# Constants at the ends of stages, half the batches normalised in the adding stage, and changed orders in five stages

## The chip, the cores and the metric

The kernel runs on one core of a Trainium2 chip. The metric is the device time of one execution in microseconds (us). The core's engines are PE (TensorE, matrix products), DVE (VectorE), ACT (ScalarE), POOL (GpSimd) and SP (SyncE, which issues most transfers). Each runs its own list and waits on semaphores. A difference of about 0.5% can be told from none.

## The reference

Twelve sublayers act on x of 8 batches × 128 tokens × 256 channels, float32, with a layer norm without weights ahead of each:

```
for layer in 0..3:
    x = x + attn(layernorm(x))
    x = x + cross_attn(layernorm(x), ctx)
    x = x + ffn(layernorm(x))
```

The sublayers differ. What the change touches of them:

```
# L0 ffn
x_dq = clip(round(x * scale_x), -128, 127) / scale_x         # per token
w_dq = clip(round(w / gamma_w), -1, 1) * gamma_w
bit_linear = x_dq @ w_dq.T + b
out = bit_linear(silu(bit_linear(x, gate)) * bit_linear(x, val), out)
# L2 cross attention: per head of 16 channels
q = ln(x @ Wq + bq); k = ln(ctx @ Wk + bk); softmax(q k / 4) v
# L3 attn: a state space layer with 64 heads, chunks of 128
L = exp(where(i >= j, cs_i - cs_j, -inf)); Y = sum_j (C_i . B_j) L_ij dt_j x_j ; (Y + D x) * silu(z) -> rms norm -> W_out
# L3 ffn: 8 experts of 1,2,3,4,1,2,3,4 chunks of 128 hidden units, and a shared one
h = x @ down; every expert on every token, masked h for experts not chosen
out = sum_e gate_e * (gelu(gelu(h_e) @ w1_e + b1_e) @ w2_e + b2_e) + 0.1 * shared; out @ up + gelu(x) @ core
```

## The kernel before

All of x lies in SBUF for the whole run. Each sublayer is a stage (L0a, L0x, L0f, L1a … L3f: attention, cross attention, feed forward), a block of its own in which every engine has a list written by hand; at the end of a stage all engines meet at a barrier, and semaphores are cleared. The order of work on each engine is that in which the code is written.

A stage begins with `Norm` (line 120). DVE aggregates the statistics of 8 batches (L152), ACT takes the root (L203), DVE the reciprocal and the negative mean (L187, L189), and then ACT scales batches 0, 1, 2, 6 (L212) and DVE 3, 4, 5, 7 (L147). PE turns each batch with two 128x128 transposes (L240), and ACT and DVE copy them out (L219, L181). While PE waits, it multiplies a constant by the identity into an unused bank (`idle`, L225): two products 512 columns wide at the start and narrower ones between the first batches. Where the stage before adds its result to x on DVE in four parts of two batches, `measure` (line 260) puts the statistics of the two batches behind each add (L264). `Norm.tensor` and these adds stand around every stage boundary.

In L0f (line 1113) the weights are ternary and x is rounded to integers. Eight batches run through a loop: PE makes gate and value (L1195), DVE scales them and adds the biases (L1312, L1322), ACT applies silu (L1246), DVE multiplies (L1343), takes the absolute maximum (L1345) and the scales, ACT rounds (L1268, L1272), PE turns and multiplies by the output weights.

In L2x (line 2220) queries and keys of eight batches are centred (L2370), squared, summed (L2349), given a reciprocal root (L2301 on ACT) for batches 0 to 3 and 4 to 7, normalised (L2358) and turned on PE (L2266) in two halves. ACT copies the keys (L2326) and DVE the queries (L2365).

In L3a (line 2498) a loop runs over 32 pairs of heads. Per pair PE adds a causal mask to four banks (`differences`, L2671: the identity times a 128x512 mask, and L2675: products of 32 rows that add the differences of cumulated steps), ACT takes their exponential (L2813), DVE multiplies (L2930), and PE forms the projections of a later pair as three products of rounded halves (L2728), the outputs y (L2690), transposes (L2740) and the sum over pairs in banks 0 to 3 (L2701), which stands half before and half behind the differences.

In L3f (line 3273) a hidden unit is one product of a 128x128 block of w1 with 512 tokens (L3362, plain float32), n counts units, and unit n uses bank n%4 of four. ACT applies gelu from the bank (L3451), PE multiplies by w2 (L3400) and DVE weighs by the gates and sums (L3502). Before unit 4 PE forms what experts give for a masked h (L3372), turns the idle weights (L3379) and multiplies them (L3385), and DVE starts the sum with that (L3491).

## Time and profile before

| | us |
|---|---|
| median of 3 runs | 1903.01 (1902.84 to 1909.08) |
| the profiled execution | 1902.77, its span 1901.0 |
| mean granted TensorE clock in the span | 0.952 |
| PE / DVE / ACT / POOL busy | 1667.9 / 1177.0 / 921.2 / 449.8 |
| the L3a loop | about 445 of the span (1110 to 1555) |
| L0x, L0f and L3f begin at | 111.8, 247.8 and 1780.1 |

Busy shares are means over twelve stages with different limits, so each place is read by its timeline. A granted clock of 0.50 means 1.2 GHz, 1.00 means 2.4 GHz. A matmul record's end is modelled; the distance between starts tells what a product costs. A plain float32 product 512 columns wide stands as two records.

### The profile page before, as it was taken

Reading aid. Unit: us, or ns where it says so; the run is one execution under the profiler, and the core shown is the slowest. Engines: PE = TensorE matmul, PEld = TensorE weight load, DVE = VectorE, ACT = ScalarE, POOL = GpSimd, SP = SyncE. Lnnn points to the kernel's source line nnn. Section 1 sums busy time; section 2 is a strip of 40 time slices with the busy share of each in tenths; the row PEclk is TensorE's granted clock in tenths of the full one; section 3 lists DMA queues with packets and bytes.
Section 4 is the critical chain, followed back from the end, with each engine's and each line's share of the span. In section 5 each row is a group of like instructions: output and inputs, shape, how many; then the busy total and the mean of one; then the engine's idle time right before and its main releaser. Section 6 shows DMA issues by size and latency. Waiting matters only on the chain. (4 is left out here: it accounts for less than half of the span.)

```text
span 1901.0 us, 37141 instructions
## 1 busy us (share of the span) xinstructions
PE 1667.9 (88%) x13775; PEld 1293.5 (68%) x13778; DVE 1177.0 (62%) x2317; ACT 921.2 (48%) x1953; POOL 449.8 (24%) x501
## 2 busy tenths in 40 slices
PE   7978855789999799976878879999999988999898
PEld 4766733558888646643667647777777766888676
DVE  3676688656666612226545678888888865666622
ACT  2445576246666411111344456767676644555432
POOL 1020011023333032221300224545445530000200
PEclk9999977899999999998989989999999989999899
DMA  2020000300010172221000000101010112110000
GB/s 101 3 92 3 4 30 27 118 18 26 25 33 25 68 317 44 46 50 38 15 2 28 18 17 26 33 25 33 25 33 25 28 39 100 34 33 25 1 1 22
DMA packets 27679, 77.58 MB, mean 41 GB/s; under 512 B 2992, under 2 KB 14896, under 8 KB 25392
## 3 DMA queue, kind: packets, MB, share of 16 engines
q1 hardware_dynamic: 23488, 70.91, 10.9%
q0 software_dynamic: 4080, 5.13, 1.7%
q8 instruction: 77, 1.26, 0.3%
q14 instruction: 34, 0.28, 0.0%
HBM read 62.75 MB, written 13.28 MB: 40 GB/s over the span
## 5 line engine op out<-in xcount | busy, mean ns | idle before, releaser
L2575 DVE SCALAR_TENSOR_TENSOR arena<-bank,arena 128x508 f32<-128x508 f32 (+2 forms) x204 | 151.5, 743 | 27.9 <-ACT arena L2571 15.6
L2701 PE MATMUL bank<-L3a_wo,L3a_y_gated 128*128 128x256 f32 x512 | 124.0, 386 | 0.0
L2930 DVE TENSOR_TENSOR L3a_decays<-L3a_decays,L3a_cb_masked 128x512 f32<-128x512 f32 x128 | 94.7, 802 | 43.4 <-ACT L3a_decays L2813 43.4
L225 PE MATMUL bank<-const 128*128 128x512 f32 (+1 forms) x156 | 79.6, 644 | 42.5 <-PEq L65 42.5
L2813 ACT ACTIVATE L3a_decays<-bank 128x512 f32<-128x512 f32 x128 | 66.1, 602 | 97.0 <-PE bank L2675 97.0
L2728 PE MATMUL bank<-L3a_xnT_high,L3a_w_high 128*128 128x512 f32 x256 | 105.8, 413 | 1.5 <-ACT L3a_decays L2813 1.5
L2701 PEld LDWEIGHTS bank<-L3a_wo,L3a_y_gated 128*128 128x128 f32 x512 | 92.4, 190 | 17.6 <-issue 7.3
L2728 PE MATMUL bank<-L3a_xnT_high,L3a_w_low 128*128 128x512 f32 x256 | 99.8, 390 | 0.0
L2728 PE MATMUL bank<-L3a_xnT_low,L3a_w_high 128*128 128x512 f32 x256 | 99.7, 389 | 0.0
L1932 PE MATMUL bank<-L1f_experts,xnT 128*128 x184 | 84.6, 604 | 0.9 <-DVE xnT L2035 0.7
L3027 POOL TENSOR_TENSOR arena<-arena 128x1024 f32<-128x1024 f32 x32 | 81.3, 2541 | 14.7 <-ACT arena L2820 14.7
L1983 ACT ACTIVATE arena<-bank 128x512 f32<-128x512 f32 x23 | 13.8, 598 | 141.2 <-PE bank L1932 141.2
L225 PEld LDWEIGHTS bank<-const 128*128 128x128 f32 x156 | 32.4, 230 | 69.7 <-issue 69.7
L787 ACT ACTIVATE L1x_p<-bank,L1x_minus_max,L1x_q_scale 128x128 f32<-128x128 f32 x128 | 56.7, 453 | 31.9 <-DVE L1x_minus_max L1780 31.9
L2690 PE MATMUL bank<-L3a_decays,L3a_dtx 128*64 128x128 f32 x1024 | 67.2, 279 | 3.9 <-ACT arena L2850 2.1
L2690 PEld LDWEIGHTS bank<-L3a_decays,L3a_dtx 128*64 128x64 f32 x1024 | 54.8, 136 | 22.0 <-ACT arena L2850 17.8
L787 ACT ACTIVATE L3x_p<-L3x_masked_scores,L3x_minus_max 128x128 f32<-128x128 f32 x128 | 49.6, 389 | 37.8 <-DVE L3x_minus_max L3264 37.8
L3034 POOL TENSOR_TENSOR L3a_wo<-arena 128x256 f32<-128x256 f32 x32 | 33.8, 1057 | 143.1 <-PE bank L2701 143.1
L2029 DVE TENSOR_TENSOR L1f_hidden<-arena,bank 128x512 f32<-128x512 f32 x23 | 15.8, 687 | 82.2 <-PE bank L1932 82.2
L2571 ACT ACTIVATE arena<-bank,arena 128x512 f32<-128x512 f32 x68 | 52.9, 782 | 25.1 <-PE bank L2728 25.0
L1893 POOL DMA_INDIRECT rows_added<-L1f_y,L1f_token x23 | 35.8, 1555 | 110.5 <-DVE L1f_y L2048 107.6
L632 POOL TENSOR_TENSOR x<-x,arena 128x256 f32<-128x256 f32 x48 | 32.6, 715 | 124.0 <-ACT xn L212 108.7
(612 smaller groups left out, 4641.2 us busy)
## 6 DMA issues: line engine op xcount, KB each, us to landing
arena<-in_L3p SPq DMA_DIRECT2D x32, 388.0 KB, 3.0
L1f_experts<-in_L1f SPq DMA_DIRECT2D x8, 1536.0 KB, 19.7
arena<-in_L1x SPq DMA_DIRECT2D x18, 384.0 KB, 3.0
arena<-in_L3x SPq DMA_DIRECT2D x18, 384.0 KB, 3.0
arena<-in_L0f SPq DMA_DIRECT2D x1, 4224.0 KB, 13.2
arena<-in_L3f SPq DMA_DIRECT2D x1, 4055.0 KB, 12.3
rows_sent<-L1a_blank SPq DMA_DIRECT2D x1, 2967.0 KB, 11.2
xnT<-rows_sent SPq DMA_DIRECT2D x23, 129.0 KB, 2.0
```

The lines of the kernel that those rows point to most:

```text
L225: self.nc.tensor.matmul(self.k.ps[bank][:, 0:width], self.k.ident, self.k.const[:, 0:width], start=True, stop=True)
L787: ins = nc.scalar.activation(self.p[:, h, b * P:(b + 1) * P], src[:, b * P:(b + 1) * P], ACT.Exp, bias=self.nb[:, h, b:b + 1], scale=scale ...
L1893: nc.gpsimd.indirect_dma_start(k.sums[:, :], bass.IndirectOffsetOnAxis(token[:, t % 5:t % 5 + 1], 0), y[:, t % 3, :], None, compute_op=ALU ...
L1932: mm = nc.tensor.matmul(ps[2 * (t % 2) + m][:, :], rowsT[:, t % 2, kc, :], experts[:, bass.ds(first + (m * KC + kc) * I, I)], start=(kc == 0),
L2571: return nc.scalar.activation(dst, psum, ACT.Identity, bias=bias, scale=w3)
L2575: return nc.vector.scalar_tensor_tensor(dst[:, :, d:], psum[:, :, 0:P - d], wcol, dst[:, :, d:], ALU.mult, ALU.add)
L2690: mm = nc.tensor.matmul(bank("y", half)[h * HD:(h + 1) * HD, b * P:(b + 1) * P], dtx[:, o, g, h, :], dec[:, o, h, g, :], start=True, stop= ...
L2701: mm = nc.tensor.matmul(ps[g // 2][:, (g % 2) * C:(g % 2 + 1) * C], yg[:, o, g * P:(g + 1) * P], wo[:, o, :], start=False, stop=False, ski ...
L2728: mm = nc.tensor.matmul(bank(name, half)[:, :], wm[a][:, kc, :], (xh, xl)[b][:, kc, half * HALF:(half + 1) * HALF], start=(kc + at == 0), ...
L2813: nc.scalar.activation(d4[:, n * HALF:(n + 1) * HALF], bank("d", n)[:, :], ACT.Exp).then_inc(S["diff_read"], 1)
L2930: nc.vector.tensor_tensor(d, d, cbm[:, 4 * half:4 * half + 4, :].rearrange("p b t -> p (b t)"), ALU.mult).then_inc(S["dec_ready"], 1)
L3027: nc.gpsimd.tensor_tensor(sqsum, sqsum, ysq, ALU.add).then_inc(S["sq_added"], 1)
```

## The change

It has seven parts.

1. `measure` aggregates as well. With `early` (the stages L0a, L1x, L2a, L2x, L2f, L3x) DVE aggregates all eight batches between its adds, and before the last part it takes the reciprocal and bias for batches 0 to 3; ACT (`normalise_first`) takes their root and scales these four in the adding stage. The next stage scales 4 and 6 on ACT and 5 and 7 on DVE. Elsewhere the batches of earlier parts are aggregated early and nothing is scaled.
2. `Norm.tensor` has one wide constant product at the start and none between batches; PE gets constant products as its last work in L0a, L0x, L2x (4) and L1x, L3x (5).
3. L0f: the value's bias is added by PE, as a K=64 product per half in front of the value's products; DVE's scaling of the value multiplies by the gate in place, and the separate product is gone. The factors for that bias are formed and turned in the stage's front; the maxima and clips there are in another order. Values are prefetched by two batches instead of three.
4. L2x: batches 0 to 3 are normalised two at a time, and the queries of half 0 come before batches 4 to 7; PE has four constants between.
5. L3a: the four mask products per pair become 16 tiles of 32 rows and 32 columns in bf16, of 128 to 512 columns; the wait for their banks moves to the sixth of eight output products.
6. L3f: units of the experts from the third on are three products of rounded halves, which POOL (w1), ACT and DVE (h) make. The router's results are taken among the units, and the sum starts from the bias alone; the products for masked h are added at the fourth expert.
7. The last wait for the output's store stands behind the clearing of the other semaphores.

```diff
+        self.measured, self.left, self.early = measured, k.left, k.early
+        self.rows = ((4, 6), (5, 7)) if self.early else (self.BY_ACT, self.BY_DVE)
+        self.span = slice(4 if self.early else 0, NB)
...
-            self.idle(pe, 2)
+            self.idle(pe, 1 if self.measured else 2)
...
-                if self.busy and b in ((1, 2) if self.measured else (1, 2, 3, 5, 6, 7)):
+                by_dve = b in self.rows[1]
+                if self.busy and not self.measured and j:
                     self.idle(pe, 1, C)
-                pe.wait_ge(self.s_xn[by_dve], (self.BY_DVE if by_dve else self.BY_ACT).index(b) + 1)
+                if b in self.rows[by_dve]:
+                    pe.wait_ge(self.s_xn[by_dve], self.rows[by_dve].index(b) + 1)
...
+def measure(k, dve, sem, added, batches, early=False):
+
+    st = k.stage
+    if min(batches) == 0:
+        st.s_measured, k.left, k.early = st.sem("rows_measured"), 0, early
     dve.wait_ge(sem, added)
+    if early and min(batches) == 4:
+        s_mv, s_std, s_rstd, s_scaled = first_rows(k)
+        dve.wait_ge(s_std, 1)
+        k.nc.vector.reciprocal(k.ln_rstd[:, 0:4], k.ln_std[:, 0:4]).then_inc(s_rstd, 1)
+        dve.wait_ge(s_rstd, 1)
+        k.nc.vector.scalar_tensor_tensor(k.ln_bias[:, 0:4], k.ln_mv[:, 0:4, 0], -1.0, k.ln_rstd[:, 0:4], ALU.mult,
+                                         ALU.mult).then_inc(s_scaled, 1)
     for b in batches:
-        k.nc.vector.bn_stats(k.ln_stats[:, b, :], k.x[:, b, :])
+        k.nc.vector.bn_stats(k.ln_stats[:, b, :], k.x[:, b, :]).then_inc(st.s_measured, 1)
+    for b in range(k.left, max(batches) + 1 if early else min(batches)):
+        dve.wait_ge(st.s_measured, b + 1)
+        ins = k.nc.vector.bn_aggr(k.ln_mv[:, b, :], k.ln_stats[:, b, :])
+        if early and b == 3:
+            ins.then_inc(first_rows(k)[0], 1)
+        k.left = b + 1
+
+
+def normalise_first(k, act):
+
+    s_mv, s_std, s_rstd, s_scaled = first_rows(k)
+    act.wait_ge(s_mv, 1)
+    k.nc.scalar.activation(k.ln_std[:, 0:4], k.ln_mv[:, 0:4, 1], ACT.Sqrt, bias=k.c["ln_eps"]).then_inc(s_std, 1)
+    act.wait_ge(s_scaled, 1)
+    for b in range(4):
+        k.nc.scalar.activation(k.xn[:, b, :], k.x[:, b, :], ACT.Identity, bias=k.ln_bias[:, b:b + 1],
+                               scale=k.ln_rstd[:, b:b + 1])
...
+                ln.idle(pe, 4, bank=0 if a.turned else 4)
...
+        a = SmallHeads(k, st, hd, [(0, P)], 1.0 / hd ** 0.5, early=False)
...
+                    if bank:
+                        pe.wait_ge(s_bTa, 1)
+                        pe.wait_ge(s_bTd, 1)
+                        pe.wait_ge(s_parts, 2)
+                        for h in range(2):
+                            nc.tensor.matmul(ps[bank + h][:, :], backT[:, n * P:(n + 1) * P],
+                                             bias[:, h * HALF:(h + 1) * HALF], start=True, stop=False)
                     for kc in range(KC):
                         for h in range(2):
                             mm = nc.tensor.matmul(ps[bank + h][:, :], xiT[:, kc, n * P:(n + 1) * P],
                                                   t[:, kc, h * HALF:(h + 1) * HALF],
-                                                  start=(kc == 0), stop=(kc == KC - 1))
+                                                  start=(kc == 0 and not bank), stop=(kc == KC - 1))
...
+                    values(n + 2)
...
-                            v[:, n % 2, h * HALF:(h + 1) * HALF], ps[2 + h][:, :], vscale[:, n:n + 1],
-                            w["val_b"][:, h * HALF:(h + 1) * HALF], ALU.mult, ALU.add)
+                        dve.wait_ge(s_silu, n + 1)
+                        own = g[:, n % 3, h * HALF:(h + 1) * HALF]
+                        ins = nc.vector.scalar_tensor_tensor(own, ps[2 + h][:, :], vscale[:, n:n + 1], own, ALU.mult,
+                                                             ALU.mult)
...
+                    values(n)
                     dve.wait_ge(s_vread, n + 1)
-                    dve.wait_ge(s_silu, n + 1)
-                    step(nc.vector.tensor_tensor(g[:, n % 3, :], g[:, n % 3, :], v[:, n % 2, :], ALU.mult))
...
+                ln.idle(pe, 5)
...
+                pe.wait_ge(s_cent, NB)
+                ln.idle(pe, 4, bank=0)
...
-                    if b >= 5:
-                        normalised(b - 5)
+                    if b in (5, 6):
+                        normalised(2 * b - 10)
+                        normalised(2 * b - 9)
                 squared(NB - 1)
-                normalised(3)
+                queries(0)
                 for b in range(4, NB):
                     normalised(b)
-                queries(0)
...
-                        nc.tensor.matmul(bank("d", n)[:, :], identr[:, :], later[:, :, :].rearrange("p m t -> p (m t)"),
-                                         start=True, stop=False)
+
+                def differences(pe, s):
+
+                    for turn in range(4):
+                        for n in range(4):
+                            g, own = (n + turn) % 4, slice(32 * n, 32 * n + 32)
+                            out = bank("d", n)[32 * g:32 * g + 32, :].rearrange("p (b t) -> p b t", b=4)
+                            nc.tensor.matmul(out[:, :, 0:32 * g + 32], ident32[own, :],
+                                             over(later[own, g, 0:32 * g + 32], 4), start=True, stop=False,
+                                             skip_group_check=True)
...
+                        if b == part[-1] and of_next is not None:
+                            free_for_differences(pe, *of_next)
...
+                        output(pe, j - 3, 1 - s, 1, (0, 1), (j, i))
+                    elif not first:
+                        free_for_differences(pe, j, i)
                     if not first:
-                        differences(pe, j, s, i)
+                        differences(pe, s)
                     if not early(j, 3):
-                        output(pe, j - 3, 1 - s, 1)
+                        output(pe, j - 3, 1 - s, 1, (2, 3))
...
+                    tok = slice(half * HALF, (half + 1) * HALF)
+                    if first[e] < ROUNDED:
+                        nc.tensor.matmul(ps[n % 4][:, :], w1[:, first[e] + c, :], gh[:, tok], start=True,
+                                         stop=True).then_inc(s_up, 1)
+                        return
+                    own = slice((first[e] + c - ROUNDED) * P, (first[e] + c - ROUNDED + 1) * P)
+                    pe.wait_ge(s_w1l, (own.stop - 1) // part + 1)
+                    pe.wait_ge(s_ghl, 2)
+                    for at, (m, r) in enumerate(THREE):
+                        mm = nc.tensor.matmul(ps[n % 4][:, :], (w1h, w1l)[m][:, own], (ghh, ghl)[r][:, tok],
+                                              start=(at == 0), stop=(at == 2))
+                    mm.then_inc(s_up, 1)
...
+                    if n == 4:
+                        pe.wait_ge(s_d, 1)
+                    if n in (14, 15):
+                        pe.wait_ge(s_itc, n - 13)
+                    if n in (22, 23):
+                        pe.wait_ge(s_corr, n - 21)
+                    hidden(e, c, half, n)
                     if e and c == 0 and half == 1:
                         out(e - 1)
+                        if e <= 3:
+                            (idle_outputs, lambda: None, turn_idle)[e - 1]()
+                        if e == 4:
+                            correct()
...
+                    if n not in (4, 8, 14):
+                        act.wait_ge(s_up, n + 1)
                     if e >= 2:
                         act.wait_ge(s_y, 2 * (e - 2) + 2)
+                    if n == 4:
+                        r.exponent(act)
+                        act.wait_ge(s_dp, 1)
+                        nc.scalar.activation(d[:, :], ps[0][0:E, 0:P], ACT.Copy).then_inc(s_d, 1)
+                        act.wait_ge(s_up, n + 1)
+                    if n == 8:
+                        act.wait_ge(s_gd, 1)
+                        nc.scalar.activation(gexp[:, :], gdiff[:, :], ACT.Exp).then_inc(s_ge, 1)
+                        act.wait_ge(s_up, n + 1)
+                    if n == 14:
+                        for m in range(2):
+                            act.wait_ge(s_it, m + 1)
+                            nc.scalar.activation(idleT[:, m * HALF:(m + 1) * HALF], ps[2 + m][0:E, :],
+                                                 ACT.Copy).then_inc(s_itc, 1)
+                        act.wait_ge(s_up, n + 1)
...
+                    if e == 3:
+                        for half in range(2):
+                            dve.wait_ge(s_c, half + 1)
+                            dve.wait_ge(s_yr, 2 * (e - 1) + half + 1)
+                            own = acc[:, 4 * half:4 * half + 4, :]
+                            nc.vector.tensor_tensor(own, own, ps[2 + half][:, :].rearrange("p (b l) -> p b l", b=4),
+                                                    ALU.add).then_inc(s_corr, 1)
...
-                    for s in [*k.used, k.s_sent, k.s_added]:
+                    for s in [*(s for s in k.used if s is not k.s_out), k.s_sent, k.s_added]:
                         sp.sem_clear(s)
+                    sp.wait_ge(k.s_out, 64)
+                    sp.sem_clear(k.s_out)
```

Where it moves instructions, PE's list at the head of a pair in L3a stood so (const,L3a_xT are the transposes of the pair before; L3a_wo the sum over pairs; L3a_later the mask; L3a_diff the step differences):

```order
L2740 MATMUL bank<-const,L3a_xT 128x128 x8
L2701 MATMUL bank<-L3a_wo,L3a_y_gated 128x256 x4
L2671 MATMUL bank<-L3a_later,L3a_ident_r 128x512 x4
L2675 MATMUL bank<-L3a_diff_right,L3a_diff_left 128x512 x4
L2701 MATMUL bank<-L3a_wo,L3a_y_gated 128x256 x4
L2728 MATMUL bank<-L3a_xnT_high,L3a_w_high 128x512
L2728 MATMUL bank<-L3a_xnT_low,L3a_w_high 128x512
```

and stands so now, with seven of the 16 tiles and the last:

```order
L2839 MATMUL bank<-const,L3a_xT 128x128 x8
L2797 MATMUL bank<-L3a_wo,L3a_y_gated 128x256 x6
L2764 MATMUL bank<-L3a_later_tiles,L3a_ident 32x4x32
L2764 MATMUL bank<-L3a_later_tiles,L3a_ident 32x4x64
L2764 MATMUL bank<-L3a_later_tiles,L3a_ident 32x4x96
L2764 MATMUL bank<-L3a_later_tiles,L3a_ident 32x512
L2764 MATMUL bank<-L3a_later_tiles,L3a_ident 32x4x64
L2764 MATMUL bank<-L3a_later_tiles,L3a_ident 32x4x96
L2764 MATMUL bank<-L3a_later_tiles,L3a_ident 32x512
...
L2764 MATMUL bank<-L3a_later_tiles,L3a_ident 32x4x96
L2769 MATMUL bank<-L3a_diff_right,L3a_diff_left 128x512 x4
L2797 MATMUL bank<-L3a_wo,L3a_y_gated 128x256 x2
L2827 MATMUL bank<-L3a_xnT_high,L3a_w_high 128x512
```

Four full-height products became 16 tiles, and two of the four output products behind them now stand ahead.

PE's list at the start of L3f, from the first hidden units on, before:

```order
L302 MATMUL bank<-arena,xnT 128x8 x16
L3362 MATMUL bank<-L3f_gelu_hT,arena 128x512 x4
L3372 MATMUL bank<-arena,L3f_u_by_expert 8x128 x20
L3379 MATMUL bank<-const,L3f_idle_weights 8x128 x8
L3385 MATMUL bank<-L3f_idle_out,L3f_idle_weightsT 128x128 x8
L3400 MATMUL bank<-arena,L3f_u 128x128 x8
L3362 MATMUL bank<-L3f_gelu_hT,arena 128x512 x4
L3400 MATMUL bank<-arena,L3f_u 128x128 x16
```

and now:

```order
L341 MATMUL bank<-arena,xnT 128x8 x16
L3477 MATMUL bank<-L3f_gelu_hT,arena 128x512 x4
L3524 MATMUL bank<-arena,L3f_u 128x128 x8
L3494 MATMUL bank<-arena,L3f_u_by_expert 8x128 x20
L3477 MATMUL bank<-L3f_gelu_hT,arena 128x512 x2
L3484 MATMUL bank<-L3f_gelu_hT_high,L3f_w_high 128x512
L3484 MATMUL bank<-L3f_gelu_hT_low,L3f_w_high 128x512
...
L3524 MATMUL bank<-arena,L3f_u 128x128 x24
L3501 MATMUL bank<-const,L3f_idle_weights 8x128 x8
L3508 MATMUL bank<-L3f_idle_out,L3f_idle_weightsT 128x128 x8
```

The products for masked h (L3372, now L3494), the idle weights' transposes (L3379, now L3501) and their products (L3385, now L3508) were one block behind unit 3, and are now spread behind the outputs of experts 0, 2 and 3.

DVE's list at the end of L3x and the start of L3f, from its third add on, before:

```order
L825 TENSOR_TENSOR x<-x,bank 128x512
L264 BN_STATS ln_stats<-x 128x6 x2
L825 TENSOR_TENSOR x<-x,bank 128x512
L264 BN_STATS ln_stats<-x 128x6 x2
L3113 UNCONDITIONAL_BRANCH
L3458 UNCONDITIONAL_BRANCH
L152 BN_AGGR ln_mv<-ln_stats 128x2 x8
L187 RECIPROCAL ln_rstd<-ln_std 128x8
L189 SCALAR_TENSOR_TENSOR ln_bias<-ln_mv,ln_rstd 128x8
L147 TENSOR_SCALAR xn<-x,ln_mv,ln_rstd 128x256 x4
```

and now:

```order
L865 TENSOR_TENSOR x<-x,bank 128x512
L281 RECIPROCAL ln_rstd<-ln_std 128x4
L283 SCALAR_TENSOR_TENSOR ln_bias<-ln_mv,ln_rstd 128x4
L286 BN_STATS ln_stats<-x 128x6 x2
L289 BN_AGGR ln_mv<-ln_stats 128x2 x2
L865 TENSOR_TENSOR x<-x,bank 128x512
L286 BN_STATS ln_stats<-x 128x6 x2
L289 BN_AGGR ln_mv<-ln_stats 128x2 x2
L3215 UNCONDITIONAL_BRANCH
L3608 UNCONDITIONAL_BRANCH
L190 RECIPROCAL ln_rstd<-ln_std 128x4
L192 SCALAR_TENSOR_TENSOR ln_bias<-ln_mv,ln_rstd 128x4
```

The eight aggregates went from the new stage into the old one, two behind each pair of statistics, and one reciprocal and one bias for batches 0 to 3 with them.

## Rows read from the trace of the kernel before

**Rows 1.** The page, part 1: busy us (share of the span) xinstructions.

```profile
PE 1667.9 (88%) x13775; PEld 1293.5 (68%) x13778; DVE 1177.0 (62%) x2317; ACT 921.2 (48%) x1953; POOL 449.8 (24%) x501
```

**Rows 2.** Windows: us, busy of PE, PEld, DVE, ACT, POOL, then clock, DMA.

```profile
1110.00:1555.00 445.00, 436.87 (x2807) 346.37 (x2806) 354.71 (x510) 295.26 (x409) 213.53 (x213) 1.00 0.09 26
1780.00:1784.00 4.00, 3.93 (x6) 1.79 (x7) 2.30 (x14) 2.37 (x5) 0.49 (x2) 0.50 0.03 6
1068.50:1075.50 7.00, 6.27 (x24) 3.71 (x25) 3.79 (x18) 3.58 (x8) 0.93 (x1) 0.76 0.34 117
```

**Rows 3.** Timeline, boundary L3x|L3f: start, us, engine, line, tiles [idle before <-releaser].

```profile
1780.07 3.75 PE L225 MATMUL bank<-const 128*128 128x512 f32 x4 [4.84 <-PEq L65]
1780.07 0.64 DVE L152 BATCH_NORM_AGGREGATE ln_mv<-ln_stats 128x2 f32<-128x6 f32 x8 [0.64 <-PEq L65]
...
1781.52 2.07 ACT L212 ACTIVATE xn<-x,ln_bias,ln_rstd 128x256 f32<-128x256 f32 x4 [0.47 <-DVE ln_bias L189]
...
1783.61 0.63 PE L240 MATMUL bank<-const,xn 128*128 128x128 f32 x2
...
1788.05 0.67 PE L3354 MATMUL bank<-xnT,arena 128*128 128x512 f32 x1 [0.72 <-ACT xnT L219]
```

**Rows 4.** Timeline, the last projections of L0a and L0x and the stages behind.

```profile
102.59 7.08 PE L476 MATMUL bank<-arena,L0a_on_by_token 128*128 128x256 f32 x32
...
238.19 7.17 PE L476 MATMUL bank<-arena,L0x_on 128*128 128x256 f32 x32
...
247.79 0.64 DVE L152 BATCH_NORM_AGGREGATE ln_mv<-ln_stats 128x2 f32<-128x6 f32 x8 [0.91 <-PEq L65]
```

**Rows 5.** Timeline, one batch of the loop of L0f.

```profile
284.34 1.22 DVE L1343 TENSOR_TENSOR L0f_g<-L0f_g,L0f_v 128x1024 f32<-128x1024 f32 x1
...
287.42 1.24 ACT L1268 ACTIVATE L0f_h_rounded<-L0f_g,L0f_magic,L0f_h_scale 128x1024 f32<-128x1024 f32 x1 [1.96 <-DVE L0f_h_scale L1348]
...
290.57 1.21 DVE L1343 TENSOR_TENSOR L0f_g<-L0f_g,L0f_v 128x1024 f32<-128x1024 f32 x1
```

**Rows 6.** Timeline, the second half of L2x's normalisation.

```profile
953.31 2.97 PE L2266 MATMUL bank<-const,arena 128*128 128x128 f32 x13 [2.46 <-DVE arena L2358]
...
957.34 0.32 ACT L2301 ACTIVATE L2x_rstd<-L2x_var 128x128 f32<-128x128 f32 x1
...
957.69 2.50 DVE L2358 TENSOR_TENSOR arena<-arena,L2x_rstd 128x512 f32<-128x512 f32 x4 [4.44 <-ACT L2x_rstd L2301]
...
961.73 3.65 PE L2266 MATMUL bank<-const,arena 128*128 128x128 f32 x16 [5.45 <-DVE L2x_qT L2365]
```

**Rows 7.** Timeline, PE in a pair of L3a.

```profile
1202.05 0.58 PE L2728 MATMUL bank<-L3a_xnT_high,L3a_w_high 128*128 128x512 f32 x1
1202.48 0.39 PE L2728 MATMUL bank<-L3a_xnT_low,L3a_w_high 128*128 128x512 f32 x1
1202.70 0.39 PE L2728 MATMUL bank<-L3a_xnT_high,L3a_w_low 128*128 128x512 f32 x1
...
1212.46 1.28 PE L2671 MATMUL bank<-L3a_later,L3a_ident_r 128*128 128x512 f32 x4
1213.67 0.51 PE L2675 MATMUL bank<-L3a_diff_right,L3a_diff_left 32*128 32x512 f32 x4
```

**Rows 8.** Timeline, PE: 32-row products in L0a, full-height ones in L3a.

```profile
89.79 1.17 PE L407 MATMUL bank<-L0a_km,L0a_qT 32*128 32x128 f32 x32
...
1209.95 1.09 PE L2740 MATMUL bank<-const,L3a_xT 128*128 128x128 f32 x8
```

**Rows 9.** Groups of L3f: line, shapes xcount | busy us, mean ns | idle before.

```profile
L3362 PE MATMUL bank<-L3f_gelu_hT,arena 128*128 128x512 f32 x84 | 39.1, 616 | 0.0
```

**Rows 10.** Timeline, PE behind the router's results in L3f.

```profile
1806.78 2.05 PE L3385 MATMUL bank<-L3f_idle_out,L3f_idle_weightsT 8*128 8x128 f32 x16 [0.93 <-DVE L3f_idle_weightsT L3488]
...
1809.61 3.57 PE L3400 MATMUL bank<-arena,L3f_u 128*128 128x128 f32 x16 [0.78 <-DVE L3f_acc L3491]
```

**Rows 11.** Waits of SP at the end: us, times, longest.

```profile
SPq L3325 <- DMA out_x<-x: 2.0, 1, 2.0
```

219 lines of the change are left out of this document (131 added, 88 removed).

## The prediction

> **What bounds the kernel now.** I read the page first: PE is busy for 88% of the span, DVE for 62%, ACT for 48% [rows 1]. The windows then show that the rest is not spread evenly. Over the whole span the granted TensorE clock is 0.952; in the long loop of L3a it is 1.00 and PE is busy in 436.9 of 445 us, while windows just behind a stage's start have 0.50 [rows 2]. So three kinds of place have to be priced: L3a's loop, where PE's own work is the time; the stage boundaries, where PE waits for the layer norm and then runs at half clock; and loops that another engine bounds (L0f, by DVE) or a chain of waits (L2x, start of L3f). All sums are made against the profiled execution, 1902.8 us (span 1901.0), which stands 0.2 us below the median 1903.0.
>
> **Boundaries.** At L3x|L3f [rows 3] the stage starts at 1780.07 (DVE waited 0.64, so its statistics ended at 1779.4), two constant 512-column products (four instructions) hold PE for 3.75 us, the eight aggregates take 0.64, ACT scales four batches in 2.07, the first transposes start at 1783.61, and the stage's own first matmul at 1788.05: a front of 8.0 us. In the changed kernel the aggregates (0.64), a second reciprocal and bias (0.20+0.17) and about 0.4 of waiting for ACT's root enter DVE's add-and-measure chain, which is the last thing to end there: +1.45. PE had waited 4.84 when the stage began; five constants of 3.75/4×2 = 1.88 at half clock, 0.94 at full, are 4.7 if warm and lie under that wait and the longer chain. The front loses the aggregates and two of the four scalings: batches 4 to 7 are scaled at about +2 (root, reciprocal and bias 0.9, then two of the 0.52 scalings), their eight transposes end at +2.6, two copies at +3.9, first matmul at about +4.1. 8.0−4.1−1.45 = 2.4 us gained, of which about 1.8 is the constants at the warm clock. L1x|L1f has the same order of work and the same edit: 2.4. L2f|L3a and, like it, L2a|L2x have fronts of 7.0 at a mean clock of 0.76 [rows 2] and no constants behind the stage: the front falls to 4.0, the chain grows by 0.6 (DVE has gaps there since PE paces the adds): 2.4 each. At L0a|L0x PE's projection runs until 109.67 and four warm constants end at 113.3, or with the clock at half at 117, while the barrier fell at 111.8 [rows 4]: the end grows by 1.5, the front shrinks by 3.2: 1.7. L2x|L2f gets four constants at its end for a front that was the shortest: 0.1. The three boundaries where only some aggregates move (L0f|L1a, L1a|L1x, L1f|L2a) give 0.3, 1.4 and 0.8 by 0.08 for each aggregate and one constant less. L0x|L0f gets four constants behind a projection that ends at 245.4 (238.19+7.17), where DVE's chain ended at 246.9 [rows 4]: 245.4+3.5, +2.0 at the end, 0.9 back in the front, so 1.1 **lost**. Sum of boundaries: 4×2.4+1.7+0.1+2.5−1.1 = **12.8**. Ends: nothing kept but the aggregates (4), or all fronts warm (17).
>
> **L0f.** The batch period is 6.23 us (284.34 to 290.57) and DVE shows no idle time in it; ACT waits 1.96 in each for DVE's scale [rows 5]. The change takes the 1.22 us product g·v away (the value's scalar_tensor_tensor now multiplies instead of adding the bias) and gives PE two K=64 matmuls per batch, 0.23 to 0.43 each, in a loop in which PE waits for DVE: hidden. ACT, busy for 6.23−1.96 = 4.3, is the next bound, under the new 5.01. Seven periods × 1.22 = **8.5**. The added front work (eight transposes, two copies on ACT and DVE, POOL's two passes) could cost up to 2.5 before the first gate; reordered clips take about as much off the same path. Range 6 to 9.
>
> **L2x.** The second half of the normalisation starts late for one reason [rows 6]: ACT's root for batches 4 to 7 stands at 957.34 behind ACT's copies of the first half, which wait for PE's transposes of the first half, which waited 2.46 us for DVE. DVE then waits 4.44, does four normalisations (2.50) and only then the queries (1.5), and PE starts the second half's transposes at 961.73, at half clock (3.65 for 16). With batches 0 to 3 normalised two at a time at b=5 and 6 and the queries of half 0 ahead of the rest, the root comes at about 953.5 (3.8 earlier), the queries no longer stand in PE's way (1.5), and the constants keep the clock (1.8): **7.0**. If the clock stays low and the constants themselves are in the way (4×0.94) it is 4; the most is 9.
>
> **L3a.** This is the term that is hard to price. Per pair the four full-height identity·mask matmuls take 1.21 us (1212.46 to 1213.67), 32 groups [rows 7]; PE hardly waits, and DVE is busy in 354.7 of the 445 us [rows 2], so what they save is saved whole. The 16 tiles that replace them move 4×(128+256+384+512) columns. No row shows a 32-row, 32-column tile. The nearest are the 32-row products with 128 columns: 32 in 1.17 us, 0.037 each, where eight full-height ones with 128 columns take 1.09, 0.136 each [rows 8]: row groups overlap by 3.7, and short instructions are issued that fast. At 0.43 ns a column (0.227 for 512 [rows 7]) a row group's own 1280 columns are 0.55; in the order of turns, with each tile behind its row group's last, I count 1536 columns to the end, 0.65; if every turn waits for its longest, 2048, 0.87. Over these lies the cost of changing the tile shape: the first full-height product after the output's takes 0.43 instead of 0.227 [rows 7], so 0.2. That gives 0.85 to 1.07, and 0.91 is taken: 0.30 saved × 32 = **9.6**. Bounds: nothing overlaps, 5120 columns = 2.2 us, +1.0 each, 32 **lost**; ideal, 0.65, 18 gained.
> The row of 0.43 is a first product behind a change of tile shape. The Trainium skill, "TensorEngine Tiling (Array Packing)", section Key Properties, says that changing the tiling mode drains the engine, and the change adds one such switch per pair; by that rule alone 32×0.2 = 6.4 us come off the gain. The same skill, "TensorE: Matmul & The Clock Gate", gives about 62 ns per matmul where hardware decode is off, which would make 16 tiles 1.0 us; the 0.037 of rows 8 does not agree with that case here.
> The wait for free banks now stands ahead of the sixth output product rather than between products 4 and 5: nothing is queued on PE that could go past it in either place, and it was met long before. The masks now come with L3a's weight image, 0.28 MB more: 0 to +2 in that front, 0 taken.
>
> **L3f.** 36 of the 42 hidden units (84 instructions of 39.1 us, 0.93 a unit with the ones at half clock, 0.87 at the full one) become three rounded products at 0.227, 0.68: 36×0.187 = 6.7 [rows 7, 9]. PE's waits for the idle weights (0.93) and the accumulator (0.78) [rows 10] go, 1.7, since router results are taken later; Against it: PE waits for ACT's copy of the idle output at unit 4 (about 0.7), ACT gets two copies of the high half and two more table loads of 1.28 while PE can run only four banks ahead, about 1.5. Splitting w1 is six passes on POOL behind L3f's bias adds; the first pair ends some 2 us ahead of unit 6. **6.5**, from 3 to 9.
>
> **End.** The wait for the output's store, 2.0 us [rows 11], now lies beside the clearing of semaphores: **1.7**.
>
> Sum: 12.8+8.5+7.0+9.6+6.5+1.7 = 46.1. 1902.8−46.1 = 1856.7; with 0.2 to the median **1857**.
>
> **Rivals.** (a) *Mask tiles save nothing.* The switch of tile shape, or turns that wait for their longest member, make the group 1.2 us again: 1857+9.6 = 1866.5. For it: rows 7's 0.43. Against: rows 8. (b) *Constants at the ends are in the way.* PE's clock may have fallen by then (it is 0.50 in windows at each boundary [rows 2]) and four constants cost 6.9 rather than 3.5 us. At five places +2 each: 1867 (for it also the 3.75 us of rows 3). Against: the projections ahead of them run warm. (c) *Mask tiles run one by one*, 2.2 us: 1857+9.6+32 = 1898.6, within 0.5% of no change. (d) *The other side*: the same 16 tiles on PE in L3a, if each has to leave the array before the next goes in. Without the masks' gain the kernel stands at 1866.5; it comes back to 1903 when a group costs 1.21+36.5/32 = 2.35 us, 0.147 per tile, and at the 0.136 to 0.17 that full-height instructions of 128 columns take, with a little for each change of column group, 16×0.17 = 2.7 us, +1.5 in 32 pairs, it is 1915. Against: rows 8, where products on neighbouring row groups are issued at 0.037. (e) *The clock gives more*: fronts warm everywhere and L2x at its best, 1857−11 = 1846. (f) *The change doesn't do what it says in L3f*: units ahead of the router wait for ACT's two table loads or POOL's split; 3 rather than 6.5, L0f's front +2.5: 1863.
>
> **How the numbers follow.** Forecast 0.40; (a) 0.16, (b) 0.15, (e) 0.11, (f) 0.08, (c) 0.05, (d) 0.02, and 0.03 for a part that stalls in a way no row shows (about 1885). The range takes in the forecast, (a), (b), (e) and (f): 1843 to 1878. A measurement of this kernel can tell about 0.5%, 9.5 us, from no change: faster means below 1893.5. All cases but (c) and (d) are faster: 0.93; (c) is the same: 0.05; (d) slower: 0.02.
>
> **What would show it.** In L3a, 0.9 us from the start of the first tile to the start of the differences, and a pair period shorter by 0.3. At L3x|L3f, a front of 4.1 with first transposes within 1 us. In L0f, a period of 5.0. In L2x, transposes of half 1 in under 2 us, some 5 us earlier in the stage. In L3f, 0.68 per unit and no wait of PE over 1 us. The prediction is wrong if the mask group takes over 1.2 us, if the barrier waits for PE's constants at more than two stages, or if DVE or ACT shows no slack in L3a's pairs.

## The result, and the profile after

The changed kernel takes **1873.74 us** (median of 4 runs, 1872.17 to 1875.61) beside 1903.61 for the kernel before (4 runs): ratio 0.9842, 95% interval 0.9828 to 0.9856. That is 29.9 us less where 46.1 were forecast: the direction and the range held, and 16 us of the forecast gain did not come. The profiled execution took 1872.17 us, span 1870.0, mean granted clock 0.955 (before 0.952).

The page of the changed kernel, part 1 (busy us, share of the span, instructions; compare [rows 1]):

```profile
PE 1655.7 (89%) x14220; PEld 1276.5 (68%) x14220; DVE 1175.1 (63%) x2316; ACT 931.7 (50%) x1979; POOL 461.8 (25%) x510
```

PE lost 12 busy us while the span lost 31: most of what came off was waiting. The stages say where. Each time runs from the first instruction behind one barrier to the first behind the next, in the two profiled executions; the forecast column is the prediction's terms put together by stage. Below, the front of a stage is the time from its start to its first own product, and the period of a loop is the time from one round to the next.

| stage | before | after | change | forecast |
|---|---|---|---|---|
| L0a | 103.0 | 104.3 | +1.3 | +1.5 |
| L0x | 136.0 | 131.8 | −4.2 | −1.2 |
| L0f | 77.2 | 74.0 | −3.2 | −9.4 |
| L1a | 66.4 | 71.5 | +5.1 | −0.3 |
| L1x | 265.8 | 266.0 | +0.2 | 0 |
| L1f | 200.2 | 200.4 | +0.2 | −3.9 |
| L2a | 63.3 | 62.7 | −0.6 | −0.2 |
| L2x | 118.2 | 108.7 | −9.5 | −10.0 |
| L2f | 29.7 | 30.2 | +0.5 | +0.5 |
| L3a | 494.5 | 487.6 | −6.9 | −12.6 |
| L3x | 217.1 | 217.0 | −0.1 | +1.4 |
| L3f and end | 120.9 | 106.9 | −14.0 | −12.0 |

Four stages fall short: L0f by 6.2, L1a by 5.4, L1f by 4.1, L3a by 5.7. Three give more than forecast: L0x 3.0, L3f 2.0, L3x 1.5. Stages that an experiment doesn't touch still differ between profiles (L1a 68.5 to 69.1 in most of them and 71.4 in this one and another, L2a 59.7 to 63.0, L3x 217.1 to 220.5, L3a 487.4 to 490.2), so one stage in one profile is good to about 3 us. A profiled execution also lies up to 10 us from its kernel's median. What a run gained in all is therefore read from medians and ratios, and the profiles say where.

**The boundary** works as forecast. Timeline of the changed kernel at L3x|L3f (start us, us, engine, line, out<-in, count, idle before; compare [rows 3]):

```profile
1762.13 0.30 DVE L289 BATCH_NORM_AGGREGATE ln_mv<-ln_stats 128x2 f32<-128x6 f32 x2
...
1763.07 0.30 ACT L206 ACTIVATE ln_std<-ln_mv,const 128x4 f32<-128x4 f32 x1 [0.99 <-PEq L66]
...
1763.10 1.10 PE L228 MATMUL bank<-const 128*128 128x512 f32 x2 [1.67 <-PEq L66]
1764.03 1.91 PE L244 MATMUL bank<-const,xn 128*128 128x128 f32 x16
1766.66 1.52 PE L3467 MATMUL bank<-xnT,arena 128*128 128x512 f32 x3 [0.72 <-ACT xnT L222]
```

The last aggregates lie ahead of the barrier, the first transposes start 0.96 behind it (3.54 before), and the stage's first product stands at 3.59 instead of 7.98; 4.1 was forecast. L3a's front fell from 6.99 to 3.57 in the same way.

At three other boundaries, L0a|L0x, L0x|L0f and L2x|L2f, PE's constants were the last thing to end: when the new stage began, PE had been idle for 0.6, 0.9 and 0.6 us, and DVE for 2.2, 2.7 and 1.4. DVE waited 1.6, 1.8 and 0.8 for them. The prediction expected this at the first two, and named more than two such stages as a sign of being wrong.

**L0f** shows the forecast period, and a delay in front of it that was not in the sum. The changed kernel's DVE and POOL at the stage's start, and two batches of the loop:

```profile
245.82 1.88 POOL L1222 TENSOR_TENSOR L0f_val_b_parts<-arena,const 64x1024 fp32r<-64x1024 f32 x1
245.92 1.81 DVE L192 SCALAR_TENSOR_TENSOR ln_bias<-ln_mv,ln_rstd 128x8 f32<-128x8 f32 x1
247.66 2.75 DVE L150 TENSOR_SCALAR xn<-x,ln_mv,ln_rstd 128x256 f32<-128x256 f32 x2
...
247.79 2.47 POOL L1224 TENSOR_TENSOR L0f_val_b_parts<-arena,L0f_val_b_parts 32x1024 fp32r<-32x1024 f32 x1
...
268.28 1.39 DVE L1395 SCALAR_TENSOR_TENSOR L0f_g<-bank,L0f_gate_scale,arena 128x512 f32<-128x512 f32 x2
...
289.13 1.22 DVE L1424 TENSOR_REDUCE L0f_gamma_h<-L0f_g 128x1 f32<-128x1024 f32 x1
...
294.24 1.22 DVE L1424 TENSOR_REDUCE L0f_gamma_h<-L0f_g 128x1 f32<-128x1024 f32 x1
```

The period is 294.24−289.13 = 5.11 (6.23 in [rows 5]; 5.01 forecast). But an operation on 8 columns takes 1.81 where it takes 0.17 without company, and ends with POOL's first pass; ACT's scalings wait for it. The first gate comes 23.2 behind the stage's start, 18.4 before.

**L2x** gave nearly what was forecast. The changed kernel's second half (compare [rows 6]):

```profile
948.49 3.60 PE L228 MATMUL bank<-const 128*128 128x512 f32 x8
...
950.24 0.31 ACT L2386 ACTIVATE L2x_rstd<-L2x_var 128x128 f32<-128x128 f32 x1
...
951.47 2.49 DVE L2444 TENSOR_TENSOR arena<-arena,L2x_rstd 128x512 f32<-128x512 f32 x4
...
954.02 1.64 PE L2348 MATMUL bank<-const,arena 128*128 128x128 f32 x13 [0.27 <-DVE arena L2444]
```

The root stands 30.6 behind the stage's start (919.63) instead of 36.7, and the transposes of half 1 start at 32.8 to 34.4 instead of 41.1; 13 of them take 1.64, 0.13 each, where 16 took 3.65, 0.23 each.

**L3a.** PE in a pair of the changed kernel, with DVE and ACT in the loop that goes through them (compare [rows 7]):

```profile
1400.53 2.77 PE L2797 MATMUL bank<-L3a_wo,L3a_y_gated 128*128 128x256 f32 x12
1403.23 0.42 PE L2764 MATMUL bank<-L3a_later_tiles,L3a_ident 32*32 32x128 bf16 x16
1403.59 0.51 PE L2769 MATMUL bank<-L3a_diff_right,L3a_diff_left 32*128 32x512 f32 x4
...
1412.73 1.45 PE L2839 MATMUL bank<-const,L3a_xT 128*128 128x128 f32 x8
1414.10 2.85 PE L2797 MATMUL bank<-L3a_wo,L3a_y_gated 128*128 128x256 f32 x12
1416.88 0.42 PE L2764 MATMUL bank<-L3a_later_tiles,L3a_ident 32*32 32x128 bf16 x16
```

```profile
1404.20 2.07 ACT L2913 ACTIVATE L3a_decays<-bank 128x512 f32<-128x512 f32 x4 [2.92 <-PE bank L2769]
...
1412.83 0.63 ACT L2952 ACTIVATE L3a_xT<-arena 128x512 f32<-128x512 f32 x1 [1.18 <-DVEq L3070]
```

```profile
1404.83 2.92 DVE L3032 TENSOR_TENSOR L3a_decays<-L3a_decays,L3a_cb_masked 128x512 f32<-128x512 f32 x4 [1.35 <-ACT L3a_decays L2913]
1407.90 2.30 DVE L2662 SCALAR_TENSOR_TENSOR arena<-bank,arena 128x508 f32<-128x508 f32 x3 [0.16 <-ACT arena L2658]
1410.44 2.30 DVE L2662 SCALAR_TENSOR_TENSOR arena<-bank,arena 128x508 f32<-128x508 f32 x3 [0.24 <-DVE arena L2662]
```

The 16 tiles take 1403.59−1403.23 = 0.36 to the start of the differences, where 0.91 was taken in the sum and 1.21 was the time before. Yet the period is 1416.88−1403.23 = 13.65, hardly shorter than the 13.69 before (1213.67 back to 1199.98). Through the loop 13.48 and 13.65 alternate, 13.57 in the mean: 0.12 shorter than before, where 0.30 was forecast. The eight transposes take 1.45 to run instead of 1.09: the second four wait for ACT's copy of 1412.83, which waited for DVE's taps (to 1412.74), these for DVE's products, these for ACT's exponentials, and these for the differences of this very pair. PE is busy for 422.7 of 437 us here, the loop's first pairs with their longer waits included:

```profile
1103.00:1540.00 437.00, 422.72 (x3165) 322.99 (x3164) 354.00 (x514) 289.79 (x405) 208.34 (x213) 0.99 0.09 27
```

Taken over the whole stage, the front up to the first projection fell from 22.57 to 19.20 (−3.4), and the rest from 471.9 to 468.4 (−3.5, where 9.6 was forecast).

### The profile page after: what moved, and what is told of

Same layout as the page of the kernel before. It is cut to its first block and busy times, and to the rows that moved or that the text cites. A ratio compares the mean times of both kernels' runs of the same rounds, so it can differ in the third digit from the quotient of the medians.

```text
span 1870.0 us, 38238 instructions
## 1 busy us (share of the span) xinstructions
PE 1655.7 (89%) x14220; PEld 1276.5 (68%) x14220; DVE 1175.1 (63%) x2316; ACT 931.7 (50%) x1979; POOL 461.8 (25%) x510
## 5 line engine op out<-in xcount | busy, mean ns | idle before, releaser
L2662 DVE SCALAR_TENSOR_TENSOR arena<-bank,arena 128x508 f32<-128x508 f32 (+2 forms) x204 | 151.5, 743 | 18.4 <-DVE arena L2662 6.6
L228 PE MATMUL bank<-const 128*128 128x512 f32 (+1 forms) x154 | 73.7, 619 | 33.7 <-PEq L66 33.7
L3129 POOL TENSOR_TENSOR arena<-arena 128x1024 f32<-128x1024 f32 x32 | 86.3, 2695 | 44.4 <-ACT arena L2920 44.4
L1689 POOL TENSOR_TENSOR L1x_q_squares<-L1x_qT 128x512 f32<-128x512 f32 x32 | 36.6, 1161 | 101.6 <-ACT L1x_qT L1802 101.6
L2952 ACT ACTIVATE L3a_xT<-arena 128x512 f32<-128x512 f32 x64 | 40.2, 628 | 37.8 <-DVEq L3070 37.8
## 6 DMA issues: line engine op xcount, KB each, us to landing
arena<-in_L3f SPq DMA_DIRECT2D x1, 4055.0 KB, 12.8
```

The costliest lines, as they stand in the source:

```text
L228: self.nc.tensor.matmul(self.k.ps[bank][:, 0:width], self.k.ident, self.k.const[:, 0:width], start=True, stop=True)
L2662: return nc.vector.scalar_tensor_tensor(dst[:, :, d:], psum[:, :, 0:P - d], wcol, dst[:, :, d:], ALU.mult, ALU.add)
L2952: nc.scalar.activation(xT[:, s, t], conv[:, s, 4 * half:4 * half + 4, :].rearrange("p b t -> p (b t)"), ACT.Silu).then_inc(S["x_ready"], 1)
L3129: nc.gpsimd.tensor_tensor(sqsum, sqsum, ysq, ALU.add).then_inc(S["sq_added"], 1)
```

## Experiments

The ratios are to the kernel before, run on the same chip beside each. The changed kernel stands at 0.9842 (0.9828 to 0.9856).

### L3a: mask and order apart

Four kernels make a table of two edits. e1 puts the wait and the differences back behind four output products; e2 gives the full masks back in the new order; e3 has both; e5 has the old order with the wait behind most of the fourth product.

```
# e1
-                        output(pe, j - 3, 1 - s, 0)
-                        output(pe, j - 3, 1 - s, 1, (0, 1), (j, i))
+                        output(pe, j - 3, 1 - s, 0, range(4), (j, i))
...
-                        output(pe, j - 3, 1 - s, 1, (2, 3))
+                        output(pe, j - 3, 1 - s, 1)
# e2
-                    for turn in range(4):
-                        for n in range(4):
...
+                    for n in range(4):
+                        nc.tensor.matmul(bank("d", n)[:, :], identr[:, :],
+                                         later[:, :, :].rearrange("p m t -> p (m t)"), start=True, stop=False)
# e5: e1, and its fourth product in two parts, with the wait between them
+                        for c0, c1 in (((0, C - 32), (C - 32, C)) if last else ((0, C),)):
+                            if c0:
+                                free_for_differences(pe, *of_next)
```

> The changed kernel (1873.7 us), but in L3a only four of the eight output products stand ahead of the mask tiles, as before the change, instead of six. Theory A (a chain closes the loop: differences 1403.59 -> ACT's exponentials -> four DVE products -> six taps of DVE until 1412.74 -> ACT's copy -> PE's transposes -> the output products -> mask tiles): two products fewer (0.9 us) lie on that chain, the tiles start when DVE has read the two banks (1402.3 rather than 1403.23), the pair period falls from 13.57 to about 13.1, where PE itself is full, and the time by 12 to 15, to 1860. Rival B (PE's own work sets the period): the same products on the same engine, 1873.7, period 13.57. Rival C (DVE sets it): no change either, and DVE's idle time per pair stays at 2.1 us.

> The changed kernel with the four full-height identity by mask products per pair back in place of the 16 tiles, and the new place of the output products kept (six ahead). A group costs 1.21 us rather than 0.35. Theory A (chain): all 0.86 is on the chain, period 13.57+0.86 = 14.4, 1873.7+27 = 1901. Rival B (PE's own work): the same 0.86 on PE; A and B differ in the wait of PE for ACT's copy, which A keeps (0.4 per pair) and B lets vanish. Rival C (DVE sets the period): up to 0.4 of it hidden, 1886 or less.

> The changed kernel with both parts of the change in L3a undone: full-height masks, and output products split four and four. With the two runs beside it this makes a two by two table of masks and order. Theory A (the new order takes back most of what the tiles give): period 13.69 as in the kernel before, about 4 us over the changed kernel: 1878. If instead the tiles alone were worth only 0.12 per pair and the order nothing, e1 is 1873.7 and e2 is 1878 too.

> The changed kernel with four output products ahead of the mask tiles as in e1, but the wait for the four banks stands behind all but 32 columns of the fourth product, not ahead of the whole of it. In e1 PE waited 0.36 to 0.48 for DVE's read of the second bank and then did 0.63 of product before the tiles, so that the period was 13.75 and L3a took 496 (487.6 in the changed kernel). Theory A (chain through DVE; where the wait stands decides): the tiles follow DVE's read by about 0.4, 0.8 earlier against the transposes than in the changed kernel; period 13.1 to 13.3, L3a 474 to 480, time 1862 to 1867. Rival B (the order alone is bad, whatever the wait): L3a 490 or more, 1876 or more.

| | mask tiles | full masks |
|---|---|---|
| wait ahead of the 6th product | changed: 487.6 | e2: 505.2 |
| wait ahead of the 4th | e1: 496.0 | e3: 514.6 |
| wait in the 4th, ahead of its last 32 columns | e5: 485.4 | |

(us of stage L3a; before: 494.5, with full masks, behind the 4th product, one wait ahead of each bank.) The medians: e1 1878.78, ratio 0.9868 (0.9851 to 0.9884); e2 1893.35, 0.9951 (0.9934 to 0.9967); e3 1898.29, 0.9976 (0.9966 to 0.9987); e5 1874.24, 0.9836 (0.9823 to 0.9850).

The mask tiles are worth 17.6 us in the one order and 18.6 in the other, 0.55 to 0.58 a pair; by the ratios of the medians it is 21 in both, and the order is worth 5 in both (e1 against the changed kernel, e3 against e2). The starts of PE's instructions, as means of 18 pairs (the 11th to the 28th), show where the time of a pair goes:

| us, start to start | before | changed | e2 | e1 | e3 | e5 |
|---|---|---|---|---|---|---|
| eight transposes | 0.93 | 1.34 | 1.35 | 0.93 | 0.93 | 0.93 |
| output products ahead of the masks (how many) | 1.56 (4) | 2.74 (6) | 2.47 (6) | 2.52 (4) | 2.25 (4) | 2.23 (4) |
| masks | 1.21 | 0.36 | 1.21 | 0.36 | 1.21 | 0.36 |
| differences and the products behind them | 2.08 | 1.26 | 1.27 | 2.08 | 2.08 | 2.08 |
| projections and y | 7.92 | 7.87 | 7.87 | 7.90 | 7.91 | 7.91 |
| period | 13.69 | 13.57 | 14.15 | 13.79 | 14.37 | 13.50 |

**Why 0.85 less in the mask group is 0.57 less in the pair.** The records at the edge of the group, in e2 (window 1412.20 to 1412.25) and then in the changed kernel (1403.10 to 1403.25, with the first six of the tiles):

```profile
1411.93 0.38 PE L2793 MATMUL bank<-L3a_wo,L3a_y_gated 128*128 128x256 f32 x1
1411.96 0.58 PE L2761 MATMUL bank<-L3a_later,L3a_ident_r 128*128 128x512 f32 x1
```

```profile
1402.92 0.38 PE L2797 MATMUL bank<-L3a_wo,L3a_y_gated 128*128 128x256 f32 x1
1403.23 0.39 PE L2764 MATMUL bank<-L3a_later_tiles,L3a_ident 32*32 32x128 bf16 x6
```

Records of output products follow each other at 0.216. The first full-height mask is recorded 0.03 behind the last of them, and the second mask 0.42 behind the first: 0.445 for the two, which is 0.216 and 0.229. So 0.19 of the 1.21 belongs to the output product, and four masks cost 1.02. The first tile stands 0.31 behind the last output record, 0.09 more than 0.216. That is the price of going over to the tiles; between the last full-height mask and the differences, where the type stays and the shape changes, it is 0.09 as well. The Trainium skill, "TensorEngine Tiling (Array Packing)", Key Properties, says that changing the mode drains the engine; the trace agrees with these 0.09 and shows no more. 1.02−0.36−0.09 = 0.57. The 0.43 in [rows 7], from which the prediction took 0.2 for such a change, is this same early start: neither product there changes the tile shape (both are 128*128).

**What the new order costs.** The period of e2 is 0.46 longer than before with the same masks, and 0.42 of it is in the transposes: PE waits there for ACT's second copy. Six products instead of four stand ahead of the differences, so the chain from differences to exponentials to DVE to that copy starts 0.91 later (2.47 for 1.56), while PE reaches the transposes 0.86 sooner behind the differences. In the kernel before, the copy ended only 0.26 ahead of the fifth transpose, the first that needs it.

**What the old order costs.** With four products ahead (e1, e3, e5) the transposes don't wait, but PE meets DVE's read of the banks. PE in e3, then in e1:

```profile
1417.57 0.69 PE L2793 MATMUL bank<-L3a_wo,L3a_y_gated 128*128 128x256 f32 x2 [0.51 <-DVE L3a_dtx L3074]
```

```profile
1420.53 1.51 PE L2797 MATMUL bank<-L3a_wo,L3a_y_gated 128*128 128x256 f32 x6
1422.39 0.69 PE L2797 MATMUL bank<-L3a_wo,L3a_y_gated 128*128 128x256 f32 x2 [0.36 <-DVE L3a_dtx L3079]
1423.02 0.42 PE L2764 MATMUL bank<-L3a_later_tiles,L3a_ident 32*32 32x128 bf16 x16
```

DVE's read of the bank ends only then, and the whole last product stands behind that wait. The kernel before waits per bank, directly ahead of each mask, and met one wait of 0.9 there in 31 pairs; in the pair of [rows 7] its second mask started 0.47 behind the end of the read. e3 differs from it in L3a by this wait, and has a period 0.68 longer. e5 puts 32 columns behind the wait instead of 256. The view prints no wait of a PE product there, but the load of the weights shows one:

```profile
1421.89 1.28 DVE L3081 TENSOR_TENSOR L3a_dtx<-bank,L3a_dt_pair 128x512 f32<-128x512 f32 x2
```

```profile
1423.50 0.30 PEld L2799 LDWEIGHTS bank<-L3a_wo,L3a_y_gated 128*128 128x128 f32 x2 [0.44 <-issue]
```

The read ends at 1423.17 and PE goes on 0.33 later. So in e5 too the loop is closed by DVE: from the differences to the end of DVE's read it is 12.48 in the kernel before, e1, e3 and e5 alike, and from there to the next differences 1.31 in e1, 1.89 in e3 and 1.02 in e5, which add up to their periods. The stage of e5 is 2.2 shorter than the changed kernel's, within what a profile can tell, and in the medians the two can't be told apart. The 1860 expected of e1 and the 1862 to 1867 of e5 were both missed. A wait directly ahead of the tiles wasn't tried; an estimate from these rows is 12.48+0.33+0.36 = 13.2 a pair, about what PE's own work would then take (13.69−0.57 = 13.1).

### L3f: rounded products

```
# e4
-                    if first[e] < ROUNDED:
+                    if True:
```

> The changed kernel with all hidden units of L3f as one plain float32 product again (the rounded halves are still made, and not used). Theory: 36 units cost 0.87 rather than 0.68: +6.7, 1880.4. Rival: PE's pace in L3f was by now set by ACT's gelu (0.69 per unit) or by DVE's weighing, so that less than 4 comes back, 1877; or the splits on POOL, ACT and DVE were in the way and it is more than 8.

Median 1879.64, ratio 0.9881 (0.9864 to 0.9897); the stage takes 112.8, 5.9 more than in the changed kernel. Two of PE's groups in L3f of the changed kernel (count | busy us, mean ns | idle before):

```profile
L3484 PE MATMUL bank<-L3f_gelu_hT_high,L3f_w_high 128*128 128x512 f32 x36 | 15.1, 420 | 0.3 <-ACT L3f_idle_weightsT L3598 0.3
...
L3477 PE MATMUL bank<-L3f_gelu_hT,arena 128*128 128x512 f32 x12 | 7.4, 764 | 0.4 <-ACT L3f_idle_out L3589 0.4
```

Busy times of neighbouring products overlap, so the stage time is the measure: 5.9 for 36 units, 0.16 each, where 0.187 was forecast. Putting the units ahead of the router leaves waits of 0.4 and 0.3, so the part of rival (f) that has ACT's table loads stall PE there falls.

### L0f and L1a: POOL beside DVE

e6 moves POOL's two passes of L0f behind the rounding of x. e10 lets them wait for the last of DVE's scaled batches, and lets POOL's 5 us memset of L1a wait for the whole norm.

```
# e6                                    # e10
+ ln.read(pool)                         + pool.wait_ge(ln.s_xn[1], 4)   # ahead of L0f's passes
+ pool.wait_ge(s_xi, 1)                 + ln.done(pool)                 # ahead of L1a's memset
```

> The changed kernel, with POOL's two passes over the 64x1024 bias parts of L0f moved behind the rounding of x. In the changed kernel they run at 245.8 to 250.3, while DVE's bias of the norm takes 1.81 (0.17 before the change) and its four scalings 3.40 (1.38 before). Theory: DVE is held up by POOL's passes over SBUF; the front is 3.7 shorter, L0f 74.0 -> 70.3, time 1870. Rival 1: the DVE ops are long because they wait for something else at that place (their times stay as they are): 1873.7. Rival 2: the passes hold up what now runs beside them (scales and copies at 261 to 266) by as much as they took before: under 1 gained.

> The changed kernel with POOL's work in two fronts moved away from DVE operations that copy or scale from SBUF to SBUF: in L0f the two passes over the bias parts begin when DVE's four scalings are over and so lie beside its three reductions; in L1a the 5.04 us memset begins when the transposed x is copied. Theory (POOL and such a DVE operation exclude each other for a whole instruction; e6 moved it to other victims): in L0f bias and scalings are at 0.17 and 1.38 again, a clip is held up by about 1, and x is rounded 2 to 3 earlier; L0f 74 -> 71.5. In L1a DVE's four scalings fall from 5.3 to 1.4 and the front by 3 (8.3 to 5), L1a 68.6 to 71.5 -> 66. Time 1867 to 1869. Rival for L0f: reductions are held up as well, nothing gained. Rival for L1a: PE's clock falls later instead and half of it is lost again.

e6: 1874.97, ratio 0.9837 (0.9824 to 0.9851): nothing gained. The four scalings are back at 1.38 and x is rounded 3.7 earlier, but the passes now meet other operations of DVE. DVE and POOL of e6:

```profile
258.33 1.88 POOL L1224 TENSOR_TENSOR L0f_val_b_parts<-arena,const 64x1024 fp32r<-64x1024 f32 x1 [11.85 <-DVE L0f_x_int L1373]
258.47 1.78 DVE L1377 COPY L0f_by_scale<-L0f_by_scale_high 128x8 f32<-128x8 f32 x1
260.29 2.35 POOL L1226 TENSOR_TENSOR L0f_val_b_parts<-arena,L0f_val_b_parts 32x1024 fp32r<-32x1024 f32 x1
...
260.49 2.19 DVE L1379 TENSOR_TENSOR L0f_by_scale<-L0f_by_scale_full,L0f_by_scale_high 128x8 f32<-128x8 f32 x1
```

Two operations on 8 columns take 1.78 and 2.19, each to the end of the POOL instruction beside it, and both stand ahead of the first gate, which comes only 1.0 earlier.

e10: 1867.19, ratio 0.9813 (0.9794 to 0.9832); L0f takes 70.5 (74.0) and L1a 64.4 (68.5 to 71.4). Its passes lie beside reductions, which aren't held: they take 0.94 for one and 1.67 for two, as they do in the changed kernel with no pass beside them.

```profile
247.59 0.17 DVE L192 SCALAR_TENSOR_TENSOR ln_bias<-ln_mv,ln_rstd 128x8 f32<-128x8 f32 x1
247.67 1.38 DVE L150 TENSOR_SCALAR xn<-x,ln_mv,ln_rstd 128x256 f32<-128x256 f32 x4
...
249.13 1.89 POOL L1223 TENSOR_TENSOR L0f_val_b_parts<-arena,const 64x1024 fp32r<-64x1024 f32 x1 [1.60 <-DVE xn L150]
...
250.23 1.67 DVE L1367 TENSOR_REDUCE L0f_gamma_x<-xn 128x3 f32<-128x768 f32 x2
```

The clip that comes next is held until the second pass ends (1.98 instead of 1.23). The first gate comes 20.3 behind the stage's start: 2.9 of the lost 4.8 is back.

In L1a the changed kernel's memset stands beside the same four scalings:

```profile
319.01 5.04 POOL L1481 MEMSET L1a_blank<- 128x5934 f32 x1 [50.08 <-POOLq L66]
...
319.92 5.30 DVE L150 TENSOR_SCALAR xn<-x,ln_mv,ln_rstd 128x256 f32<-128x256 f32 x4
```

5.30 instead of 1.38, and PE's transposes wait 1.88 for it. This stood so before the change too; e10 takes it out. PE's idle time in the front goes with it, and the granted clock in the first 8 us of L1a is 0.72 there and 0.50 in the changed kernel. In all these rows POOL holds DVE to the end of POOL's instruction when DVE scales, copies or takes two inputs from SBUF, and not when it reduces. The Trainium skill, "SBUF — State Buffer", section Who interferes with whom, has this rule (one shared pair of ports, locked for a whole instruction; reductions stay out of it), and these rows agree.

### L1a: what the constants at the front were worth

```
# e7: in the norms where only the aggregates are early
-            self.idle(pe, 1 if self.measured else 2)
+            self.idle(pe, 1 if self.measured and self.early else 2)
...
+                if self.busy and (b in (1, 2) and not self.early if self.measured else j):
```

> The changed kernel with the constant products of before (two wide ones at the start, a narrower one before batches 1 and 2) back in the fronts of L0x to L0f's kind, that is in L1a, L1x and L2a, where nothing is normalised early. Theory: in L1a the granted clock was 0.61 and then 1.00 in the first 8 us before the change, 0.50 and 0.50 after it, because PE stood idle for 1.9 us in the front beside a five us memset; L1a's first products come back from 5.6 to 4.1 us and the stage from 68.6 (71.5 in one of the profiles) to about 66.4: -2 to -5, 1869 to 1872. Rival: the clock there depends on what PE did in L0f's end, and not on the constants: 1873.7, first products 5.6 again.

PE of the changed kernel, then of e7, where L1a's own products begin:

```profile
327.34 5.63 PE L1493 MATMUL bank<-arena 128*128 128x288 f32 x16 [0.69 <-ACT xnT L222]
```

```profile
325.43 4.13 PE L1493 MATMUL bank<-arena 128*128 128x288 f32 x16 [0.72 <-ACT xnT L222]
```

The changed kernel's first 8 us of L1a have a granted clock of 0.50 and the products still run at that for a while; with the constants back it is 0.72 in the front (0.81 before the change), the products take 1.5 less, and the stage 66.8. But the median is 1880.56 (1870.78 to 1881.01), ratio 0.9874 (0.9858 to 0.9889), 7 us more than the changed kernel, where 2 to 5 less were expected. The profiled execution, 1870.8, is the fastest of the five and lies 9.8 below that median; its mean granted clock is 0.960 and that of the others 0.954 to 0.957. So the clock explains the profile's L1a, and e7 is no cure. What takes the time in the other four executions stays open, since none of them has a profile.

### L1f: a front whose gain the transfers take

```
# e8: the next weights' transfer behind the load of the third part
-                ln.sync(sp)
...
+                    if t == 2:
+                        k.after.load(sp)
```

> The changed kernel with the load of L2a's weights (1.5 MB) in L1f issued behind the first three row tiles instead of behind L1f's experts. Theory: the front of L1f became 4.4 us shorter and the scatters start 4.4 earlier, but the first rows come back only 0.9 earlier, since the scatters share the 16 DMA engines, 0.9 busy, with 15.6 MB of weights; without L2a's 1.5 MB the first row tile comes 3 to 4 us earlier, L1f 200.4 -> 197, time 1870. Rival: the scatters are bound by their own issue on POOL or by their own latency: nothing.

L1f's front fell from 8.0 to 3.6, and the first scatter was issued at 19.8 behind the stage's start instead of 24.2, but the first product that needs the scattered rows came hardly earlier. Before, changed, e8:

```profile
705.03 0.41 PE L1920 MATMUL bank<-const,xnT 128*128 128x128 f32 x2 [3.27 <-DMA xnT<-rows_sent]
```

```profile
703.77 0.66 PE L2001 MATMUL bank<-const,xnT 128*128 128x128 f32 x2 [6.95 <-DMA xnT<-rows_sent]
```

```profile
701.48 0.41 PE L2004 MATMUL bank<-const,xnT 128*128 128x128 f32 x2 [3.42 <-DMA xnT<-rows_sent]
```

PE's wait grew by 3.7 as the front shrank by 4.4. The DMA engines are 0.93 busy up to there with weights (373 GB/s in the window 656.53 to 704.00). With one load issued later the stage takes 197.4 instead of 200.4 (199.3 to 201.1 in all runs that have the load in its old place), although the first scatter is then issued at 21.4; the median is 1869.90, ratio 0.9815 (0.9802 to 0.9829).

### The constants at the ends

```
# e9, at five places
-                ln.idle(pe, 4, bank=0 if a.turned else 4)
-                ln.idle(pe, 5)
```

> The changed kernel without the constant products at the ends of L0a, L0x, L1x, L2x and L3x (4, 4, 5, 4 and 5 of them). Theory: at L0a and L0x the barrier comes 1.5 to 2 earlier; the fronts behind L0a, L1x and L3x run at half clock again, 1.5 to 2 longer each (first own product at L3x|L3f after about 5.5 instead of 3.59), and what follows at half clock in L0x costs 2 to 3 more. L1f's stage time stays 200.4, since its front ends in a wait for transfers. Sum +2 to +5: 1876 to 1879. Rival (the constants are in the way, or do nothing): 1871 to 1873.7, with fronts at full clock anyway because the projection ahead of them had warmed it.

e9: 1871.52 (1868.67 to 1877.43), ratio 0.9828 (0.9810 to 0.9847): no difference that can be told, where 1876 to 1879 were expected. Locally they do what they are for. PE of e9 at L3x|L3f:

```profile
1768.10 2.04 PE L228 MATMUL bank<-const 128*128 128x512 f32 x2 [5.94 <-PEq L66]
...
1773.68 2.81 PE L3462 MATMUL bank<-xnT,arena 128*128 128x512 f32 x6 [0.72 <-ACT xnT L222]
```

That front is 5.6 instead of 3.6 and its clock 0.63 instead of 1.00, yet L3f takes 107.2 against 106.9. The profiled execution is e9's slowest, 1877.43: in it L0x takes 133.7 (131.8), L0f 77.1 (74.0) and L2x 109.9 (108.7), near what was expected. Its other four executions took 1868.67 to 1872.80, and what they saved isn't known.

### All three cures together

> The changed kernel with what e5 (wait for the banks behind most of the fourth product, -2 in L3a), e8 (L2a's weights loaded later, -3 to -4 in L1f) and e10 (POOL's passes and memset moved, -5) do. The three lie in different stages, so their gains should add: 1873.7-2.2-3.8-5 = 1863. Rival: the granted clock's falls move with everything ahead of them and take a part back, 1866 to 1870.

e11 has the edits of e5, e8 and e10: **1862.76**, ratio 0.9788 (0.9769 to 0.9807), span 1858.1 with a clock of 0.962. It beats both kernels, by 40.4 and, from one ratio to the other, about 10 us. L0f takes 70.5, L1a 64.4, L1f 198.4, L3a 488.4; the first three carry the gain, which was expected at 1863.

## Why the prediction came out as it did

The range held partly by luck. No case that the prediction named, alone, gives 1873.7; several terms failed together, and errors of both signs partly cancelled.

- **Boundaries, 12.8.** The fronts shrank as forecast, 3.59 instead of the 4.1 worked out. But the same gain was booked where it could not arrive: in L1f (3.9) what ended last was not the front but transfers, and the profile before had the 3.27 us wait for rows_sent to say so. L0x gained 3.0 more than forecast: PE's wait for the first rows that DVE rotates was 4.66 and is 2.79, and they are turned 10.1 behind the stage's start instead of 15.3. So a wait further in shrank as well, which the front's own length didn't show; which of the earlier steps did it wasn't tested. L0a's and L0x's ends were right (+1.3 for +1.5; the stage's end +1.9 for +2.0). L2x's end waits for PE's constants too, which the 0.1 booked there didn't foresee.
- **L1a, −0.3, measured +2.2 to +5.1.** "0.3 … by 0.08 for each aggregate and one constant less" priced the constant taken away as pure gain. It had been holding up the clock: 0.81 became 0.50, and with the constants back it is 0.72 and the first products are 1.5 shorter (e7).
- **L0f, 8.5.** The loop gave 8 as forecast. "The added front work … could cost up to 2.5", set against the reordered clips and so booked at 0, was the failed step: it cost 4.8. Of this 2.9 went when POOL's passes were moved (e10): they had been priced as POOL time and not as time in which DVE stands still. The other 1.9 stayed; DVE's new operations on the bias factors stand there, but no run takes them out.
- **L2x, 7.0:** with its front the stage was to give 10.0 and gave 9.5.
- **L3a, 9.6.** The loop gave 3.5. Both halves of the term were wrong and partly cancelled. The tiles saved 0.57 rather than 0.30 a pair: the group was taken at 0.91 and measured 0.45 (0.36 and 0.09 for the change of shape), against full masks that cost 1.02 and not 1.21. "What they save is saved whole" was the step that failed. It was inferred from PE's hardly waiting, which was true: from the 11th pair on the kernel before meets no wait of PE that a view names. But two results came only just in time, ACT's copy 0.26 ahead of the transposes that need it, and DVE's read of the banks 0.47 ahead of the second mask, where PE needs 0.33. The new order put two products into the chain that leads to the copy, 0.46 a pair with full masks. "It was met long before" failed too: with the old order e1, e3 and e5 wait for DVE's read. The sign named in the prediction, no slack of ACT or DVE, was there: DVE's idle 2 us in a pair are waits inside the chain. Rival (a), masks that save nothing, comes near the size of the loop's change but has another cause; (c) and (d) are refuted by 0.36 for 16 tiles.
- **L3f, 6.5.** The stage gave 14.0 for 12.0; rounding measured 5.9 for 6.7, front and end 5.8 together, which leaves 2.3 for the order of the units, where waits saved and waits added had been set off to −0.2. **End, 1.7:** 1.4 (from the last add to x to the end, 6.91 and 5.51).
- **Rival (b)**, constants in the way by 10 us, is refuted by e9: without them no gain can be told, though the barrier waits for them at three stages. The clock that it rested on isn't 0.50 at each boundary, as was said: [rows 2] has 0.50 at one and 0.76 at another. **Rival (f)** was right about L0f's front, which grew by 4.8 rather than 2.5, and wrong about L3f.

## What to carry to other kernels

Before a shorter front is booked as a gain, ask in that stage what ends last: with the DMA engines at 0.93 a front 4.4 us shorter gave 0.2. Before work is taken off an engine that bounds a loop, measure how close the results of the other engines come to being late: here 0.57 a pair was saved on PE, ACT's copy was in time by 0.26, and after two products had been moved ahead of the result that the chain starts from, which cost 0.46 a pair, 0.12 arrived. Work put on POOL "beside" is free only while DVE isn't scaling or copying: place it beside reductions.

## What the hardware showed that was not expected

- Sixteen 32x32 tiles in bf16, 128 to 512 columns each, take 0.36 us to the next group's start, 0.022 each; going over from full-height products to them costs 0.09.
- A rounded product behind plain float32 ones is recorded 0.03 behind the start of the last of them, though that one still takes its 0.216. The distance between the first two starts of a group then holds 0.19 of the group before.
- A POOL instruction stretches a DVE operation of 0.17 us to 1.81, and four scalings of 1.38 to 5.30, each to about its own end; reductions go on.
- PE goes on 0.33 us behind the end of DVE's read that it waits for (e5), and 0.06 behind the end of ACT's copy (the changed kernel).
- The same kernel's executions differ by up to 10 us with granted clocks of 0.954 to 0.960 (e7), which makes single constants to keep PE busy hard to value from one profile.
